# A graph network's weight stage: bias added on VectorE, weights centred ahead, squares summed on ScalarE

## The reference

```python
def layer(h, params):
    W, b, g, beta = params
    h = h * norm_out
    agg = jax.ops.segment_sum(h[src], dst, num_segments=n)
    agg = agg * norm_in
    out = agg @ W + b
    out = _layer_norm(out, g, beta)          # mean and variance over the 512 features, eps 1e-5
    out = jax.nn.gelu(out, approximate=False)
    return (out, None)
h, _ = jax.lax.scan(layer, features, (Ws, bs, ln_g, ln_b))
return _layernorm(x + h, axis=-1)
```

## Time and profile before

| | us |
|---|---|
| median of 3 runs (lowest to highest) | 1296.19 (1295.29 to 1296.88) |
| the profiled execution's own time | 1297.03 |
| its span in the trace | 1295.1 |
| mean granted TensorE clock, share of full speed | 0.847 |
| busy: PE / PE weight loads | 929.8 (72%) / 722.8 (56%) |
| busy: VectorE (DVE) | 821.1 (63%) |
| busy: ScalarE (ACT) | 467.8 (36%) |
| busy: POOL | 756.4 (58%) |
| DMA | 245.82 MB, mean 190 GB/s |

### The profile page before, as it was taken

One profiled execution on the slowest core, in us unless ns is written; L12 is line 12 of the kernel. 1 busy time (PEld: TensorE's weight loads), 2 busy tenths in 40 slices (PEclk: granted clock), 3 DMA queues, 4 the chain that ended last, 5 costly groups with the idle time before them and its releaser, 6 DMA issues.

```text
span 1295.1 us, 25238 instructions
## 1 busy us (share of the span) xinstructions
PE 929.8 (72%) x5554; PEld 722.8 (56%) x5554; DVE 821.1 (63%) x1923; ACT 467.8 (36%) x759; POOL 756.4 (58%) x921
## 2 busy tenths in 40 slices
PE   7889866847978979696895895899668889920000
PEld 7776312317757768575784784778457777820000
DVE  9687688965574746555464476447624446748886
ACT  4431123004334343333433433443334433413445
POOL 3477407634556566555664664766457746658884
PEclk9888875868999989797997997999879999965555
DMA  8932489324436272635526624752367689568998
GB/s 307 376 101 46 107 300 391 111 82 121 114 129 203 93 236 83 222 105 196 174 86 205 179 82 142 223 149 89 129 203 206 205 255 361 185 190 266 318 327 295
DMA packets 118205, 245.82 MB, mean 190 GB/s; under 512 B 20130, under 2 KB 21090, under 8 KB 118142
## 3 DMA queue, kind: packets, MB, share of 16 engines
q1 hardware_dynamic: 73838, 132.54, 28.8%
q0 software_dynamic: 31680, 89.43, 24.0%
q10 hardware_dynamic: 12624, 23.14, 4.8%
HBM read 130.10 MB, written 114.96 MB: 189 GB/s over the span
## 4 chain that ended last, share of the span: by engine, by line
PE 46%; DMA 19%; DVE 11%; issue 10%; POOL 8%; ACT 3%; POOLq 1%; DVEq 1%; ACTq 0%; SPq 0%
DMA rows<-h_rows,slot 9%; PE ps_a L1881 8%; PE ps_y L1910 7%; PE ps_y L1915 7%; PE ps_y L1911 7%; DMA h_rows<-rows 4%; POOL rows L846 3%; POOL rows L767 3%; DMA rows<-h_rows,idx 3%; PE ps_y L1748 3%; PE ps_a L1728 2%; DMA constant_factors<-row_factors 2%; DVE agg_t L963 2%; PE ps_y L1906 2%; PE ps_z L1767 2%
## 5 line engine op out<-in xcount | busy, mean ns | idle before, releaser
L1881 PE MATMUL ps_a<-sel,rows 128*128 128x128 f32 x2080 | 296.0, 294 | 60.7 <-DMA rows<-h_rows,slot 43.3
L1881 PEld LDWEIGHTS ps_a<-sel,rows 128*128 128x128 f32 x2080 | 264.6, 202 | 96.2 <-issue 92.6
L767 POOL DMA_INDIRECT rows<-h_rows,slot x230 | 221.0, 961 | 91.4 <-issue 66.4
L795 POOL TENSOR_TENSOR s_lo<-agg_t,s_hi 128x512 fp32r<-128x512 f32 x122 | 157.5, 1293 | 113.3 <-ACT s_hi L1600 113.2
L1595 ACT ACTIVATE agg_t<-ps_a 128x508 f32 x260 | 155.3, 597 | 188.0 <-PE ps_a L1881 168.0
L1910 PE MATMUL ps_y<-w_all,s_hi 128*128 128x512 f32 x488 | 190.6, 391 | 1.1 <-ACT s_hi L1600 0.4
L1911 PE MATMUL ps_y<-w_all,s_hi 128*128 128x512 f32 x488 | 189.9, 389 | 0.0
L1355 DVE TENSOR_TENSOR agg_t<-ps_a,agg_t 128x4 f32 x260 | 43.0, 165 | 179.9 <-ACT agg_t L1595 169.4
L1915 PE MATMUL ps_y<-w_all,s_lo 128*128 128x512 f32 x488 | 130.4, 389 | 0.0
L1227 DVE TENSOR_SCALAR sel<-iota,by_tile 128x128 f32<-128x128 f32 x284 | 102.0, 362 | 42.7 <-PE ps_a L1870 24.9
L1400 DVE BATCH_NORM_STATS2 small<-ps_y 128x6 f32<-128x512 f32 x122 | 85.1, 698 | 66.3 <-PE ps_y L1915 66.3
(11 more groups left out here) (330 smaller groups left out, 1465.5 us busy)
## 6 DMA issues: line engine op xcount, KB each, us to landing
h_rows<-agg_t SPq DMA_DIRECT2D x2, 22528.0 KB, 65.7
h_rows<-rows SPq DMA_DIRECT2D x92, 256.0 KB, 2.0
h_rows<-rows ACTq DMA_DIRECT2D x87, 256.0 KB, 4.5
out<-agg_t SPq DMA_DIRECT2D x78, 256.0 KB, 4.4
agg_t<-in_x SPq DMA_DIRECT2D x19, 1024.0 KB, 13.4
rows<-in_Ws SPq DMA_DIRECT2D x32, 256.0 KB, 2.7
w_raw<-in_Ws SPq DMA_DIRECT2D x28, 256.0 KB, 4.4
rows<-h_rows,slot POOLq DMA_INDIRECT x230, 3.7
```

What stands on the lines that cost most here:

```text
L767: g.indirect_dma_start(out=rows[:, k, :], out_offset=None, in_=table[:, :], in_offset=bass.IndirectOffsetOnAxis(ap=slot[:, k:k + 1], axis=0))\
L795: g.tensor_tensor(s_lo[:, k, :, :], agg_t[:, :, bass.ds(c * P, P)], s_hi[:, k, :, :].bitcast(f32), ALU.subtract).then_inc(lo_ok, 1)
L1881: m = mm(ps_a[k % GS][:, b, :], rows[:, k, b * P:(b + 1) * P], sel[:, k % GS, :], start=True, stop=True)
```

## The change

Per tile, the bias product on PE goes. The weights' rows are made free of their mean over the 512 columns, so that a product with them has mean zero, and the bias has its own mean taken off; so no mean of the tile is needed. VectorE adds the bias out of PSUM into a bank `t_now` of which there is one (`add_bias`), ScalarE squares it and sums the squares over the row (`square`, result into the bank `ps_q`, sum into `squares`), POOL makes the inverse root of that, VectorE multiplies the bank by gamma into `ps_s[k]` (`by_gamma`) and then scales straight into the row buffer `made[k]`, where gelu works in place. The row means of all 32 weight chunks are made on ScalarE in the setup (`mean_of`). The bias is loaded into 128 rows.

```diff
-        b_rows = sb("b_rows", [P, D], f32r)
+        b_rows = sb("b_rows", [P, D])[:, :]
+        row_mean = sb("row_means", [P, LAYERS * KB])
-        ps_t = [ps_z[:, :], ps_f[4]]
+        ps_s, ps_q, t_now = [ps_z[:, :], ps_f[4]], ps_f[0], ps_f[1]
...
             for n in range(4, KB * LC):
                 sp.wait_ge(u_mm, n - 3)
+                sp.wait_ge(wm_ok, n - 3)
                 sp.dma_start(w_ring[n % 4], Ws[1 + n // KB, n % KB * P:(n % KB + 1) * P, :]).then_inc(uw_in[n % 4], 16)
...
-                    sp.wait_ge(w_ok, done(L * KB + KB - 1))
-                    sp.dma_start(b_raw[0:2, 0, :], bs[L, :].partition_broadcast(2)).then_inc(b_in, 16)
+                    sp.wait_ge(t_ok, done(base))
+                    sp.sem_inc(sp_tick, 1)
+                else:
+                    sp.wait_ge(wm_ok, KB * LAYERS)
+                sp.dma_start(b_rows, bs[L, :].partition_broadcast(P)).then_inc(b_in, 16)
...
             def inverse(j, k):
-                pool.wait_ge(mv_ok, done(j + 1))
+                pool.wait_ge(sq_ok, done(j + 1))
                 pool.sem_inc(tick, 1)
-                g.tensor_scalar(var[:, k:k + 1], mv[:, k, 1:2], EPS, None, ALU.add).then_inc(var_ok, 1)
+                g.tensor_scalar(var[:, k:k + 1], squares[:, k:k + 1], 1.0 / D, EPS, ALU.mult, ALU.add).then_inc(var_ok, 1)
...
-                    v.tensor_copy(w_hi[:, q, :], w_raw[:, q % 2, :]).then_inc(wh_ok, 1)
+                    mean = row_mean[:, L * KB + q:L * KB + q + 1]
+                    v.tensor_scalar(w_hi[:, q, :], w_raw[:, q % 2, :], mean, None, ALU.add).then_inc(wh_ok, 1)
                     dve.wait_ge(wh_ok, L * KB + q + 1)
-                    v.tensor_tensor(w_lo[:, q, :], w_raw[:, q % 2, :], w_hi[:, q, :].bitcast(f32), ALU.subtract)\
-                     .then_inc(w_ok, 1)
+                    v.scalar_tensor_tensor(w_lo[:, q, :], w_raw[:, q % 2, :], mean, w_hi[:, q, :].bitcast(f32),
+                                           ALU.add, ALU.subtract).then_inc(w_ok, 1)
...
-                    bias()
...
-            def centre(j, k):
...
+            def bias(L):
+
+                dve.wait_ge(b_in, (L + 1) * 16)
+                dve.sem_inc(dve_tick, 1)
+                v.bn_stats(b_now, b_rows).then_inc(b_ok, 1)
+                dve.wait_ge(b_ok, L + 1)
+                v.bn_aggr(b_mean, b_now).then_inc(bm_ok, 1)
+                dve.wait_ge(bm_ok, L + 1)
+
+            def add_bias(j, k):
+
+                dve.wait_ge(sc_made, done(j))
+                dve.sem_inc(dve_tick, 1)
                 dve.wait_ge(y_ok, done(j + 1))
+                v.scalar_tensor_tensor(t_now, ps_y[k][:, :], b_mean[:, 0:1], b_rows,
+                                       ALU.subtract, ALU.add).then_inc(t_ok, 1)
+
+            def by_gamma(j, k):
+
+                dve.wait_ge(sq_ok, done(j + 1))
                 dve.sem_inc(dve_tick, 1)
+                v.tensor_tensor(ps_s[k], t_now, gam, ALU.mult).then_inc(sc_made, 1)
+
+            def scale(j, j_pair, k):
+
+                dve.wait_ge(sc_made, done(j + 1))
                 dve.sem_inc(dve_tick, 1)
+                dve.wait_ge(h_st[k], j_pair * 8 + 16)
                 dve.sem_inc(dve_tick, 1)
                 dve.wait_ge(rs_ok, done(j + 1))
-                v.scalar_tensor_tensor(ps_t[k], ps_t[k], rstd[:, k:k + 1], bet,
+                v.scalar_tensor_tensor(made[k], ps_s[k], rstd[:, k:k + 1], bet,
                                        ALU.mult, ALU.add).then_inc(u_ok, 1)
 
             def w_stage(L, pairs, pb):
                 base, nb = pb * 2, pairs * 2
+                bias(L)
                 dve.wait_ge(gb_in, (L + 1) * 32)
                 dve.sem_inc(dve_tick, 1)
-                centre(base, 0)
+                add_bias(base, 0)
+                by_gamma(base, 0)
                 with dve.Fori(0, pairs - 1) as pair:
                     j = base + pair * 2
                     for k in range(2):
-                        centre(j + k + 1, 1 - k)
-                        scale(j + k, k)
-                scale(base + nb - 2, 0)
-                centre(base + nb - 1, 1)
-                scale(base + nb - 1, 1)
+                        add_bias(j + k + 1, 1 - k)
+                        scale(j + k, j, k)
+                        by_gamma(j + k + 1, 1 - k)
+                add_bias(base + nb - 1, 1)
+                scale(base + nb - 2, base + nb - 2, 0)
+                by_gamma(base + nb - 1, 1)
+                scale(base + nb - 1, base + nb - 2, 1)
...
+            def mean_of(n):
+
+                a.activation(b_rows, w_ring[n % 4], ACT.Copy, scale=-1.0 / D,
+                             accum_out=row_mean[:, n:n + 1]).then_inc(wm_ok, 1)
...
+            def square(j, k):
+
+                hold(t_ok, done(j + 1))
+                hold(sq_ok, done(j))
+                a.activation(ps_q, t_now, ACT.Square, accum_out=squares[:, k:k + 1]).then_inc(sq_ok, 1)
+
+            def gelu(j, k, last, at):
                 hold(u_ok, done(j + 1))
-                hold(h_st[k], j_pair * 8 + 16)
-                a.activation(made[k], ps_t[k], ACT.Gelu).then_inc(h_ok, 1)
+                a.activation(made[k], made[k], ACT.Gelu).then_inc(h_ok, 1)
...
                         high(j + k + 3, c + k + 3, 1 - k)
-                        gelu(j + k, j, k, L + 1 == LAYERS, bass.ds(within(rb + (c + k) * P, 0, ROWS - P), P))
+                        square(j + k + 1, 1 - k)
+                        gelu(j + k, k, L + 1 == LAYERS, row(c + k))
...
-                        mm(ps_y[k][:, :], ones_w[:, :], b_rows[:, :], start=True, stop=False)
                         pe.wait_ge(hi_ok, done(j + k + 1))
                         pe.sem_inc(pe_tick, 1)
                         for b in range(KB):
-                            mm(ps_y[k][:, :], s_hi[:, k, b, :], w_hi[:, b, :], start=False, stop=False)
+                            mm(ps_y[k][:, :], s_hi[:, k, b, :], w_hi[:, b, :], start=b == 0, stop=False)
```

More of the change, by code:

```diff
@@ L131, in build @@
         quads_t = slot[0:1, UN:UN + 2]
-        small = sb("small", [P, 25])
-        stats = small[:, 0:12].rearrange("p (a b) -> p a b", b=6)
-        mv = small[:, 12:16].rearrange("p (a b) -> p a b", b=2)
+        small = sb("small", [P, 27])
+        b_now, b_mean = small[:, 0:6], small[:, 12:14]
+        squares = small[:, 25:27]
         var, rstd, mhalf, zcol = small[:, 16:18], small[:, 18:20], small[:, 20:21], small[:, 21:25]
@@ L1483, in _ @@
             a = nc.scalar
-            for s in (ev_ok, hi_ok, h_ok, co_h):
+            for s in (ev_ok, hi_ok, h_ok, co_h, sq_ok):
                 act.sem_inc(s, PRIME)
@@ L1520, in _, with later_means @@
                          ps_z[:, 0:KB * LC].rearrange("p (k l) -> p k l", l=LC), ACT.Copy).then_inc(cz_ok, 1)
+            def mean_of(n):
+                a.activation(b_rows, w_ring[n % 4], ACT.Copy, scale=-1.0 / D,
+                             accum_out=row_mean[:, n:n + 1]).then_inc(wm_ok, 1)
+            def later_means(first, last):
+                for n in range(first, last):
+                    if n == 0:
+                        act.wait_ge(fill_st, 48)
+                    else:
+                        act.wait_ge(wm_ok, n)
+                    act.wait_ge(uw_in[n % 4], 16 * (n // 4 + 1))
+                    mean_of(KB + n)
+            later_means(0, CH)
             for q in range((LEVELS + 1) * CH, LOOKUPS * CH):
@@ L1537, in _ @@
             for n in range(KB):
+                act.wait_ge(wm_ok, KB * LC + n)
+                mean_of(n)
+            for n in range(KB):
+                act.wait_ge(wm_ok, KB * LC + n + 1)
+                a.activation(w_ring[n], w_ring[n], ACT.Identity, bias=row_mean[:, n:n + 1]).then_inc(wc_ok, 1)
+            for n in range(KB):
+                act.wait_ge(wc_ok, n + 1)
                 a.activation(w_hi[:, n, :], w_ring[n], ACT.Copy).then_inc(wh_ok, 1)
@@ L1611, in w_stage @@
                 base, nb = pb * 2, pairs * 2
-                hold(b_ok, done(L + 1))
                 hold(y_ok, done(base - 1))
@@ L1617, in w_stage, with row @@
                     high(base + n, n, n % 2)
+                square(base, 0)
+                def row(n):
+                    return bass.ds(within(rb + n * P, 0, ROWS - P), P)
                 with act.Fori(0, pairs - 2) as pair:
@@ L1622, in w_stage @@
                         high(j + k + 3, c + k + 3, 1 - k)
-                        gelu(j + k, j, k, L + 1 == LAYERS, bass.ds(within(rb + (c + k) * P, 0, ROWS - P), P))
+                        square(j + k + 1, 1 - k)
+                        gelu(j + k, k, L + 1 == LAYERS, row(c + k))
                 high(base + nb - 1, nb - 1, 1)
                 for n in range(4, 0, -1):
-                    gelu(base + nb - n, base + nb - n - n % 2, n % 2, L + 1 == LAYERS,
-                         bass.ds(within(rb + (nb - n) * P, 0, ROWS - P), P))
+                    if n > 1:
+                        square(base + nb - n + 1, (n + 1) % 2)
```

(3 more changed lines are left out.)

63 lines of the change are left out of this document (19 added, 44 removed).

## The result

The changed kernel takes 1283.6 us (median of 4 runs, 1283.2 to 1285.5) against 1296.4 for the kernel before on the same chip (1295.3 to 1296.9): a ratio of 0.990, 95% interval 0.987 to 0.992. The forecast was 1285, with 1275 to 1301. The profiled execution took 1283.2 us, 1281.2 of it the span.

What follows compares the result with a forecast made beforehand. TensorE's thirteen matmuls were taken as the bound, then a VectorE-ScalarE ring through one bank. Terms -15.3 - 1.8 + 6.5 - 0.9 = -11.5 from 1297.0 gave 1285.5, forecast as 1285 us (0.8 above the median); range 1275 to 1301.

Steps and rivals of the forecast that it cites:

- The ring: Layers 0 to 6: add_bias, Square, row sum, by_gamma and hand-overs through one bank set the pace, 2.77 us a tile.
- term a: Time to write out the Square's row sum on ScalarE: between 0 and 0.35 us, taken as 0.15.
- the floor of the new pace: TensorE's 12 remaining matmuls at 0.227 us each: 2.72 us per tile, 0.23 below the old pace.
- forecast of layers 0 to 6: Pace 2.77 against 2.95 us, 0.18 gained at each of 85 steps from tile to tile: -15.3 us.
- 2.77 (right): Test on the pace of add_bias rows in layer 6: 2.77 us would show the forecast right.
- rival 1: TensorE's matmuls set a pace of 2.72 and layer 7 loses half as much: -20, 1276 us; chance 0.23.
- The first product of a layer: It comes one matmul earlier in each of eight layers, 8 x 0.23: -1.8 us.
- Layer 7: Scale waits for stores, 3.75 us a tile early; ScalarE sets 3.05 later: +6.5 us, bounds 0 and +17.
- Transitions: Last tile of a layer: stores 0.6 us later in four, constants 1.3 earlier in three: -0.9, bounds -5 and +4.
- Setup: 36 added mean and centre instructions on ScalarE cost nothing; bounds 0 and +8 us.
- Rival 4: If Square is not in Gelu's table, two table loads of 1.28 us per tile: near 1485 us; chance 0.02.
- rival 2: Chain through one bank outlasts thirteen matmuls: pace 2.97, +8, 1304 us; slower from a row-sum cost of 0.29; chance 0.17.

Runs made afterwards that it cites:

- e8: The kernel before without its bias product, so 12 matmuls a tile (output lacks the bias): 0.9866 (1279.0 us).
- e1: The changed kernel with two of each tile's 12 matmuls left out: 0.9869 of the kernel before (1279.4 us).
- e9: The changed kernel with its new 128-byte tile of weight-row means allocated last in SBUF: 0.9871 of the kernel before (1279.7 us).
- e5: The changed kernel with layer 7's store wait moved from VectorE's scale back to ScalarE's gelu: 0.9864 of the kernel before (1278.8 us).
- e10: The kernel before with an unused 128-byte tile allocated ahead of s_hi: 1.0043 (1302.0 us).
- e3: The changed kernel with a second, thrown-away Square over half of the row ahead of the real one: 1.0283 of the kernel before (1333.1 us).

## Why the prediction was right, and where it was not

1. **What bounds the kernel before** was right: TensorE's thirteen matmuls. e8 proves it by taking one away.
2. **The ring.** Forecast 2.62 + a = 2.77; measured alone, in e1, 2.74. The term a came as its own row of 193 ns, but Square and read-out overlap and take 0.70 together (884.39 to 885.08), where 0.75 stood in the sum. By_gamma is 0.70 as taken; the hand-over after it is 0.22 and not 0.13.
3. **The step that failed**: "12 x 0.227 = 2.72 per tile. That is the floor of the new pace". The floor was 12 x 0.2333 = 2.80 (2.79 in the layers with a spacing of 0.2324), above the ring. So the forecast of layers 0 to 6 (-15.3; measured 251.8 - 237.0 = -14.8) came out through another bound than the one it names, and that the two numbers are so close is luck. Of the measured 14.8, 1.3 is the last step of each layer, which the forecast had counted with the last tile. Its test "2.77 (right)" fell between, 2.795 in layer 6 with VectorE waiting for PE, the sign given to rival 1. Neither rival has the cause. It lies in a line that the forecast passed over, the allocation of row_means. Nothing in the trace of before showed that a place costs time, but the change did move the operands, and that deserved a bound: 3% of 12 matmuls in 85 steps is 7 us. By e9 it costs 2.6 us in layers 0 to 6 (236.98 against 234.34), since the ring stands 0.05 below.
4. **The first product of a layer** (-1.8) did not come. From bridge to first tile it is 5.3 to 5.5 us before and 5.3 to 5.7 after; in e8, where only the bias product is gone, it is 5.30 in the mean for 5.35. The bias product ran while TensorE had to wait for s_hi anyway: the lines view has 8.8 us of that wait, for L1949, after, and 0.4 before. Ahead of that wait the matmul cost next to nothing.
5. **Layer 7**, forecast +6.5, measured +3.7. The mechanism was right (e5 takes it away), its sizes were not: the cycle, from one scale of a buffer to its next, was 7.6 to 8.4 and not 7.5, but it held for five pairs, to 1077 us, 43 us behind the first add_bias and not 54, and the late part ran at 2.94 a tile (steps of 3.17 and 2.71 by turns), not 3.05.
6. **Transitions**, forecast -0.9, measured -5.5 and -0.6 at the end. Timelines of VectorE and ScalarE at the last tile of layer 2, beside the earlier trace rows:

```profile
521.01 0.76 DVE L1398 SCALAR_TENSOR_TENSOR ps_a<-ps_y,small,b_rows 128x512 f32<-128x512 f32 x1 [0.27 <-PE ps_y L1954]
...
523.78 0.75 DVE L1414 SCALAR_TENSOR_TENSOR rows<-ps_a,small,rows 128x512 f32<-128x512 f32 x1 [0.26 <-POOL small L803]
...
524.66 0.63 ACT L1640 ACTIVATE rows<-rows 128x512 f32<-128x512 f32 x1 [1.47 <-DVE rows L1414]
```

   From add_bias to gelu that is 3.65 where 3.85 was forecast. Into layers 1 to 3 the stretch grew by 1.0 to 2.3; into layers 4 to 7 it shrank by 1.6 to 4.6 where 1.3 was forecast for three. The lines view shows where: TensorE's first constants' product waited 61.0 us in all for the factors' load, now 43.5. The kernel before,

```profile
L1870 PE MATMUL ps_y<-constant_vectors,constant_factors 10*128 10x512 f32 x38 | 20.9, 644 | 81.4 <-DMA constant_factors<-row_factors 61.0 <-DVE ps_a L1407 20.4
```

and the change:

```profile
L1912 PE MATMUL ps_y<-constant_vectors,constant_factors 10*128 10x512 f32 x38 | 19.2, 597 | 59.5 <-DMA constant_factors<-row_factors 43.5 <-DVE ps_a L1398 11.9 <-ACT rows L1603 4.2
```

   Without the thirteenth matmul but with the old order (e8) the seven stretches take 421.2 us, as before (421.6), and 416.1 after the change; so it is not the missing matmul. The kernels with the old order lie at 421.2 to 423.4 (e10), those with the change's own at 415.0 (e5) to 419.5 (e9): a gain is there, its size is known to some 3 us only. With more work in the ring (e3, 421.0) or with two banks (423.0 and 421.2) it is gone. That these loads land sooner because fewer transfers stand beside them is argued, not shown.
7. **Setup**, forecast 0 with bounds 0 and +8: +2.7, by ScalarE's wait for the ring of weights, which the text named and costed at nothing. The last eight instructions (220.07 to 225.50) were hidden, as said.
8. Rival 4 is out: no table load stands in a W stage; both kernels have four in all, of 1283 ns each. The trace has no load between Square, Copy and Gelu; by the rule of the Trainium skill ("ScalarE: Activation LUTs", "Table sets: the hidden batching unit") Square is then one of the fillers or in the set of Gelu. The threshold of rival 2, a = 0.29, leaves out what the rival itself adds in layer 7; with it the sum is zero at 0.27. Nothing hangs on it.

The errors cancel: -14.8 for -15.3, +0.6 for -1.8, +3.7 for +6.5, -6.1 for -0.9, +2.7 for 0.

## What to carry to other kernels

Before a new resource is sized, ask which engine waits for which: an engine that waits 0.37 us in each tile does not need relief, and taking one piece of the change alone (e8) shows what each piece is worth. When a change allocates a small tile, put it behind the operands of the matmuls, and compare the spacing of the matmuls' starts before and after; a few rows of the timeline are enough for it. A ring through one buffer that lies 2% below the floor is a bound in waiting: it took both edits, place and second bank, to reach 2.72.
